# Loading repeated reciprocals from another engine's DMA queue, in smaller groups, in a fused attention and mixture-of-experts kernel

## The reference

```python
x = x + attention(layernorm(x), ctx)          # ctx: 4 x 1601 x 512, 257 image rows, 1344 text rows
# attention: 16 heads of 32
q     = rms_norm(linear(x, q_w), norm_q_w)
k, v  = rms_norm(linear(ctx_txt, k_w), norm_k_w), linear(ctx_txt, v_w)
ki,vi = rms_norm(linear(ctx_img, k_img_w), norm_k_img_w), linear(ctx_img, v_img_w)
out   = linear(softmax(q k^T / sqrt(32)) v + softmax(q ki^T / sqrt(32)) vi, o_w)
x = x + moe(layernorm(x))                     # router, 32 experts, 4 per token, shared expert
```

## Time and profile before

| | us |
|---|---|
| time, median of 3 runs (lowest, highest) | 1255.73 (1253.97, 1257.35) |
| the profiled execution: its time | 1254.77 |
| the profiled execution: its span | 1253.0 |
| PE busy | 1132.6 (90%) |
| DVE busy | 823.3 (66%) |
| ACT busy | 647.8 (52%) |
| POOL busy | 194.9 (16%) |
| mean granted clock of PE | 0.976 of full speed |

### The profile page before, as it was taken

The page is one execution under the profiler, slowest core; times in us unless marked ns, Lnnn a source line. Parts: engine busy times, 40 slices in busy tenths (PEclk is TensorE's granted clock), DMA queues, the critical chain, the costliest instruction groups (busy, mean ns, idle before and its releaser), DMA issues. The chain is left out here.

```text
span 1253.0 us, 20692 instructions
## 1 busy us (share of the span) xinstructions
PE 1132.6 (90%) x8420; PEld 406.4 (32%) x8420; DVE 823.3 (66%) x1034; ACT 647.8 (52%) x916; POOL 194.9 (16%) x299
## 2 busy tenths in 40 slices
PE   7999999779999986989998699999589999999996
PEld 2442223334222233422223242222244434333332
DVE  6766779677677967867787686998468953211221
ACT  5559885334898643489864348996121111211221
POOL 1220000133000022300002240001020003222442
PEclk9999999989999998999999899999889999999999
DMA  9760002557200165720006575013753217999842
GB/s 310 167 119 22 2 2 80 127 105 195 59 2 2 49 140 110 191 76 2 2 22 160 108 191 169 2 35 108 229 216 117 84 78 268 364 303 306 245 70 31
DMA packets 142169, 152.47 MB, mean 122 GB/s; under 512 B 108528, under 2 KB 108784, under 8 KB 136048
## 3 DMA queue, kind: packets, MB, share of 16 engines
q1 hardware_dynamic: 136944, 140.22, 38.4%
q0 software_dynamic: 5120, 10.82, 4.7%
HBM read 104.06 MB, written 21.77 MB: 100 GB/s over the span
## 5 line engine op out<-in xcount | busy, mean ns | idle before, releaser
L705 ACT ACTIVATE work<-ps 128x1024 f32<-128x1024 f32 (+1 forms) x416 | 403.2, 1021 | 42.9 <-PE ps L1178 39.3
L1035 PE MATMUL ps<-wts,work 128*128 128x512 f16 x864 | 203.6, 392 | 43.7 <-DVE work L762 43.4
L1184 PE MATMUL ps<-work,vals 128*32 128x512 f32 (+2 forms) x1664 | 221.0, 603 | 1.8 <-ACT work L705 0.6
L1178 PE MATMUL ps<-quer,keys 32*128 32x512 f16 x2496 | 171.9, 377 | 19.5 <-ACT work L705 5.6
L944 DVE TENSOR_TENSOR work<-work 128x2048 f32<-128x2048 f32 x64 | 146.6, 2291 | 6.2 <-ACT work L705 0.6
L944 DVE TENSOR_TENSOR attn<-attn,work 128x2048 f32<-128x2048 f32 x62 | 142.0, 2291 | 5.5 <-ACT work L705 0.6
L1035 PEld LDWEIGHTS ps<-wts,work 128*128 128x128 f16 x864 | 85.4, 100 | 157.1 <-issue 61.8
L627 ACT CAST work<-work 128x512 f16<-128x512 f32 x68 | 42.0, 618 | 153.8 <-DVE work L794 153.8
L1989 PE MATMUL ps<-wring,xgt 128*80 128x512 f32 x256 | 114.9, 592 | 0.0
L1035 PE MATMUL ps<-wts,hl 128*128 128x512 f16 x432 | 101.1, 386 | 9.6 <-DVE wts L744 7.0
L543 POOL TENSOR_SCALAR small<-small 128x1 f32<-128x1 f32 x68 | 18.2, 268 | 581.1 <-ACT work L632 581.1
(11 more groups left out here) (209 smaller groups left out, 1277.8 us busy)
## 6 DMA issues: line engine op xcount, KB each, us to landing
wring<-in_wx SPq DMA_DIRECT2D x32, 1536.0 KB, 9.2
raw<-in_ctx SPq DMA_DIRECT2D x52, 256.0 KB, 3.3
rb<-sums_inverse SPq DMA_DIRECT2D x24, 256.0 KB, 4.5
work<-in_x SPq DMA_DIRECT2D x4, 1024.0 KB, 5.8
table<-nums SPq DMA_DIRECT2D x16, 256.0 KB, 2.5
work<-in_x SPq DMA_DIRECT2D x12, 256.0 KB, 4.9
x<-work SPq DMA_DIRECT2D x12, 256.0 KB, 2.6
x2t_rows<-nums SPq DMA_DIRECT2D x12, 256.0 KB, 2.6
```

Source lines behind the costliest of these rows:

```text
L705: act.activation(prob[0:rows, s % PROBS, 2 * half:2 * half + 2, :], ps[0:rows, 2 * pair:2 * pair + 2, :], ACT.Exp, scale=SCALE).then_inc(a ...
L1035: mm = pe.matmul(out, lhs(a, c)[:, cols], wts[:, w, z, c * D:(c + 1) * D], start=(k == 0), stop=(k == len(steps) - 1))
L1178: mm = pe.matmul(ps[:, 2 * pair + h % 2, :], k[h * HD:(h + 1) * HD, :], q[h * HD:(h + 1) * HD, :], start=(e == 0), stop=(e == len(terms) - 1))
L1184: return pe.matmul(ps[h * HD:(h + 1) * HD, NUM, :], vals[a:z, ORDER[n], g * P + h * HD:g * P + (h + 1) * HD], prob[a:z, s % PROBS, h, :], ...
```

## The change

The loads of the repeated reciprocals leave SP's order. For the batches 1 to 3 they are issued by ScalarE, one group (512 KB, four DMAs of 128 KB) at a time: groups 0 and 1 in slot 1, between `key_high(0)` and `key_square(1)`, behind a wait for the landed store; group 2 in slot 4, behind `out_high(0)`; group 3 in slot 5, behind `out_high(1)`. `out_high(g)` waits for the multiplication of group g, so the room in `rb` is free. Each of the two halves of `rb` has its own semaphore. The bytes are the same.

For the last batch SP stores the reciprocals and waits for them before the branch, and issues the eight loads at the start of the second program's block, four ahead of the router's weights and four behind. The waits for them inside the branch that is not taken are gone. Each repeated row of these loads is written as one run, 4 KB per partition in `rb` and 8 KB in `rbl`, where it was four of 2 KB.

To free a semaphore, the small loads `ob`, `vb`, `vib`, `mark` count on `s_vq`, behind a wait of SP for the two loads that used it before. `sums_inverse` has room for 4 batches instead of 8.

```diff
-            def spread_pair(bb, q, pair):
-                if pair == 0:
-                    sp.wait_ge(s_zero, 32)
-                    sp.wait_ge(s_rd, 16 * bb)
-                    upto(sp, a_at, q * NG)
-                else:
-                    sp.wait_ge(a_at, gn(q, 1))
-                spread(rb[:, :, :, :], bb - 1, pair, s_rb)
-
-            def last_spreads(bb):
-                store_sums(bb)
-                sp.wait_ge(s_rd, 16 * (bb + 1))
-                for pair in range(2):
-                    spread(rbl[:, 2 * pair:2 * pair + 2, :, :], bb, pair, s_rl[pair])
...
-                            load_vec(OB, "ob", s_vo)
+                            sp.wait_ge(s_vq, 32)
+                            load_vec(OB, "ob", s_vq)
...
-                        if i in (1, 5) and b > 0:
-                            spread_pair(bb, q, i // 4)
...
-                last_spreads(bb)
+                store_sums(bb)
+                sp.wait_ge(s_rd, 16 * (bb + 1))
...
+            def spread(bb, g):
+                for h in range(4):
+                    rows = r_dram[(bb - 1) % B][h * HD + 2 * g:h * HD + 2 * g + 2, :].rearrange("r q -> (r q)")
+                    act.dma_start(rb[h * HD:(h + 1) * HD, g % 2, :, :].rearrange("p t q -> p (t q)"),
+                                  rows.unsqueeze(0).to_broadcast([HD, 2 * L])).then_inc(s_rb[g % 2], 16)
...
+                    if b > 0 and i == 1:
+                        act.wait_ge(s_zero, 32)
+                        act.wait_ge(s_rd, 16 * bb)
+                        spread(bb, 0)
+                        spread(bb, 1)
                     if b > 0 and WEIGH + 1 <= i < WEIGH + 1 + NG:
                         out_high(q, i - WEIGH - 1)
+                        if i - WEIGH - 1 < 2:
+                            spread(bb, i - WEIGH + 1)
...
-                dve.wait_ge(s_rb, 64 * (2 * q + g // 2 + 1))
+                dve.wait_ge(s_rb[g % 2], 64 * (2 * q + g // 2 + 1))
...
+            def spread(pair):
+                for h in range(4):
+                    rows = r_dram[B - 1][h * HD + 4 * pair:h * HD + 4 * pair + 4, :].rearrange("r q -> (r q)")
+                    sp.dma_start(rbl[h * HD:(h + 1) * HD, 2 * pair:2 * pair + 2, :, :].rearrange("p g t q -> p (g t q)"),
+                                 rows.unsqueeze(0).to_broadcast([HD, 4 * L])).then_inc(s_rl[pair], 16)
+
+            spread(0)
             sp.dma_start(rraw[:, :], d["rw"]).then_inc(s_xl, 16)
+            spread(1)
             sp.dma_start(ebias[:, :], d["ebias"].partition_broadcast(P)).then_inc(s_xl, 16)
```

More of the change, by code:

```diff
@@ L387, in store_sums @@
                 sp.wait_ge(a_rcp, bb + 1)
[L388 to L394, removed]
-            def spread_pair(bb, q, pair):
-                if pair == 0:
-                    sp.wait_ge(s_zero, 32)
-                    sp.wait_ge(s_rd, 16 * bb)
-                    upto(sp, a_at, q * NG)
-                else:
-                    sp.wait_ge(a_at, gn(q, 1))
-                spread(rb[:, :, :, :], bb - 1, pair, s_rb)
-            def last_spreads(bb):
-                store_sums(bb)
-                sp.wait_ge(s_rd, 16 * (bb + 1))
-                for pair in range(2):
-                    spread(rbl[:, 2 * pair:2 * pair + 2, :, :], bb, pair, s_rl[pair])
+                sp.dma_start(r_dram[bb % B], rcp[:, :]).then_inc(s_rd, 16)
             def last_loads(p, bb):
@@ L465, in one_pass @@
                             load_weight(WO)
-                            load_vec(OB, "ob", s_vo)
-                            sp.dma_start(vb2[:, 0, :], d["vb"]).then_inc(s_vo, 16)
-                            sp.dma_start(vb2[:, 1, :], d["vib"]).then_inc(s_vo, 16)
-                            sp.dma_start(mark[:, :, :], d["mark"]).then_inc(s_vo, 16)
+                            sp.wait_ge(s_vq, 32)
+                            load_vec(OB, "ob", s_vq)
+                            sp.dma_start(vb2[:, 0, :], d["vb"]).then_inc(s_vq, 16)
+                            sp.dma_start(vb2[:, 1, :], d["vib"]).then_inc(s_vq, 16)
+                            sp.dma_start(mark[:, :, :], d["mark"]).then_inc(s_vq, 16)
                         if bb == 0 and i == 6:
@@ L560, in add_bias @@
                 if q == 0 and j == 0:
-                    pool.wait_ge(s_vo, 64)
+                    pool.wait_ge(s_vq, 96)
                 pool.wait_ge(s_xres[j % 2], 16 * (q * QT // 2 + j // 2 + 1))
@@ L903, in project @@
                     if bb == 0 and i == 12:
-                        dve.wait_ge(s_vo, 64)
+                        dve.wait_ge(s_vq, 96)
                         dve.tensor_tensor(vbias, vb2[:, 0, :], vb2[:, 1, :], ALU.add).then_inc(s_const, 1)
@@ L1304, in _ @@
             with pe.If(pe.value_load(flag[0:1, 0:1], min_val=0, max_val=1) > 0):
-                pe.wait_ge(s_vo, 64)
+                pe.wait_ge(s_vq, 96)
                 one_pass(1)
@@ L1331, in lay_attention, with ffn_program @@
     }
-def ffn_program(nc, m, d, x1_dram, table, out, s_turned, s_rl, s_gate):
+def ffn_program(nc, m, d, x1_dram, table, r_dram, out, s_turned, s_gate):
     with ExitStack() as ctx:
@@ L1366, in ffn_program @@
         s_const, s_i0 = event("s_const"), event("s_i0")
+        s_rl = [event(f"s_rl{i}") for i in range(2)]
         r_lo = event("r_lo")
@@ L2045, in build @@
         s_xr = ctx.enter_context(nc.semaphore("s_xr"))
-        s_rl = [ctx.enter_context(nc.semaphore(f"s_rl{g}")) for g in range(2)]
         s_gate = ctx.enter_context(nc.semaphore("s_gate"))
-        attention_program(nc, m, d, x1_dram, x2_dram, r_dram, table, out, s_turned, s_xr, s_rl, s_gate)
-        ffn_program(nc, m, d, x1_dram, table, out, s_turned, s_rl, s_gate)
+        attention_program(nc, m, d, x1_dram, x2_dram, r_dram, table, out, s_turned, s_xr, s_gate)
+        ffn_program(nc, m, d, x1_dram, table, r_dram, out, s_turned, s_gate)
 def kernel(**inputs):
```

13 lines of the change are left out of this document (5 added, 8 removed).

## The result

The changed kernel takes **1226.2 us** in the median of four runs (1225.1 to 1226.5), the kernel before beside it 1256.1. The ratio is 0.9765, interval 0.9752 to 0.9778: 29.5 us faster. The forecast was 1226.5. The profiled execution took 1225.96 with a span of 1224.2, 28.8 less than the span before. A total that comes out says little about the terms it is made of, so the rest of this text looks at these. Times read from one trace each scatter a little even where the code is the same: the three batches that matter last 633.0, 631.8 and 631.5 us together in the changed kernel, in e1 and in e6.

What follows compares the result with a forecast made beforehand. TensorE, busy 90% of the span, was taken to bound, idling behind loads in SP's queue. B −35.8, A +5.4 and the last batch +1.6 sum to −28.8 us: 1226.0 or 1226.9, written as 1226.5, range 1213 to 1240.

Steps and rivals of the forecast that it cites:

- What bounds: Whole kernel: TensorE, busy 90% of the span, loses time where loads from SP's queue come late.
- B: Slot 5, batches 1 to 3: earlier group 2 load removes TensorE's idle time and low clock before `key(7)`, −35.8 us.
- together at 249.4: At `key(7)`, batch 1: VectorE's work and TensorE itself both allow the start at 249.4, so nothing idles.
- A: Start of projections, batches 1 to 3: wait moves to ScalarE, delaying `key(3)`, while `ctx` tile 4 comes in time; +5.4 us.
- the issue: ScalarE's `rb` loads in slot 1: eight issues at 0.42 us each, taken from SP's four in 1.73 us.
- the low clock: TensorE after an idle stretch: twelve matmuls at the lower clock level, 4.44 us instead of 2.75 in batch 1.
- Rival 3: Batches 1 to 3: loads land no earlier, only SP's issue time is won, 12 us in all, 1244; chance 0.03.
- The last batch: Around the branch: multiply waits 5.0 us longer, earlier code fetch gives back 3.4; net +1.6, from −0.5 to +5.0.
- one sign that was named: Behind the branch: block starts 9 to 11 us after the flag, with a wait of about 5 for `rbl`.
- the bound of 5.5: Behind the branch: code fetch, if it waits for the loads, can begin up to some 5.5 us earlier.
- rival 1: ScalarE's issues cost almost nothing (0.05 us each), `key(3)` starts after 2.9 us idle: 1217; chance 0.17.

Runs made afterwards that it cites:

- e1: Changed kernel with the last batch's eight `rbl` loads back ahead of the branch on SP: 1224.66 us, ratio 0.9759 to the kernel before.
- e6: Changed kernel with four of the last batch's `rbl` loads ahead of the branch, the other four behind it: 1224.12 us, ratio 0.9753.
- e3: Changed kernel with groups 0 and 1 loaded by SP as a pair at the old place in slot 1, groups 2 and 3 on ScalarE: 1223.73 us, 0.9746.
- e5: Changed kernel with all `rb` loads on SP, one group at a time, each behind its slot's `ctx` load from slot 2 on: 1208.83 us, ratio 0.9634.
- e9: Repeat of e5, timed beside e10 on one chip in five rounds: 1206.51 us, ratio 0.9639.
- e8: Changed kernel with ScalarE's wait for the store and eight issues moved from slot 1 to slot 2, ahead of `key_high(1)`: 1216.3 us, ratio 0.9684.
- e2: Kernel before with only the last batch's loads moved behind the branch: 1254.93 us, ratio 1.0003.
- e4: Changed kernel with groups 0 and 1 issued by ScalarE as four DMAs of 256 KB instead of eight of 128 KB: 1220.19 us, ratio 0.9722.
- e7: e5 with four of the last batch's `rbl` loads ahead of the branch and four behind: 1206.47 us, ratio 0.961.
- e10: Repeat of e7, timed beside e9 on one chip in five rounds: 1202.31 us, ratio 0.9612.

## Why the prediction was right, point by point

**What bounds, and the mechanism of B.** Right. The wait for `rb` is gone, group 2 is issued in slot 4 and landed ahead of its use, and the time won at `key(7)` is carried to the end of the batch.

**The size of B, −35.8, was too large.** The step counted TensorE's idle time of the earlier trace rows as the load's. The gain ends at the first other limit: as soon as the load is early, VectorE, late by its wait at tile 4 and 3.49 us away from `key(7)` at `weigh(2)`, bounds. e3 measured −30.8. The text did say that VectorE and TensorE would arrive together at 249.4, which is why the sum came out: with A's delay on TensorE the limit does not bite, since TensorE is as late. The two terms don't add: A costs +3.2 on top of B alone (−30.8 to −27.6), and +8.2 on top of a B counted at TensorE's idle time. The +5.4 of the text stands between; and the forecast for e3, made by adding up A's share and taking it away, failed for it.

**A.** The wait, the eight issues and the engines behind them were right; `key(3)` was forecast at 226.5 and started at 227.53, 0.8 of which is the later start of the frame. Mis-sized were two: the issue (0.49 us each in this group, 0.42 taken from SP's row), and the low clock, taken as some 1.65 us for twelve matmuls, while all twelve matmuls ran low in batch 1 (5.28, 2.5 above) and nearly all in the other two (5.02 and 4.97). Taken together the batches were forecast at −30.4 (−35.8 + 5.4) and came to −27.6: the forecast was 0.7 to 1.2 us too fast in each.

**The rule on issuing engines.** The rule of the Trainium skill in "DMA: Bandwidth & Descriptors", section "Issuing engines are not separate DMA queues", is that issuing from several engines saves only the time of issue. The traces agree with half of it. Rival 3, the saving of issue time alone, is out: 12 us was its gain, 29.5 the measured. But the rule's sense, that another engine is no faster road, held better than the change: e5, with every load on SP, gains 46.0 us by its ratio. What was lost before was lost to how the loads stood in one queue's order, and what the change lost again, to the wait and the issues on an engine that others wait for.

**The last batch.** Forecast +1.6, in the trace +0.1 from flag to multiply. Both halves were too small and offset each other, which is luck: the block starts 7.0 earlier (3.4 taken; the end of the range was 5.5), and the wait for `rbl` is 7.0 (5.0 taken). So one sign that was named failed too: the block was to start 9 to 11 us after the flag and starts 5.3 after it. The step that failed is the bound of 5.5. It counts only how much earlier the fetch can begin, and that part was about right: the first instruction packets come 5.0 us earlier. The other 2.0 arise between the first packets and the block, 5.8 us before and 3.8 after; before, the first group of packets is carried beside the loads and takes until 8.5 us after the flag, 2.0 us from its first packet, where it takes 1.0 in the kernel after. Where the rest of the 2.0 arises is not shown. (SP's last issue ended 1.4 us after the flag, not 1.3; and rival 1, by its own rates, leaves 2.7 us of idle time ahead of `key(3)`, not 2.9. Neither changes a conclusion.)

**What made up the rest.** Batches at −27.6 instead of −30.4 and the last batch at +0.1 instead of +1.6 give −27.5, of a span shorter by 28.8. The 0.78 at the start and the −1.9 behind the flag close it. The latter is no effect of the change that I can show: from flag to end the twelve traces of this case have 365.6 to 373.1 us, and kernels with the same code there differ by 4.5 (e9 368.6, after 370.7, e8 373.1). Where in the experts' part this is decided was not tried. That the forecast of 1226.5 lies within 0.3 us of the time is luck: the batches gained 2.8 less than forecast, and the last batch and the 1.9 behind the flag made up for it.

## What to carry to other kernels

When a list of waits shows a wait for a DMA, look first where the load stands in its queue's order and behind which semaphore, and only then whose queue it is: a group at a time in slots 2 to 5 of SP's own order, behind the `ctx` loads, the same bytes gained 46.0 us, where another engine's queue gained 29.5. An engine that others wait for pays for every DMA that it issues and for every semaphore ahead of it, so if it must issue, let it be few and large ones. And the idle time of the bounding engine at a wait, with what the low clock behind it costs, is an upper bound of what removing this wait alone gives (35.8 counted, 30.8 measured): look up when the next engine of the chain would be ready.

## What the runs showed of the hardware

The start of a block behind a far branch depends on what the DMA engines carry: 5.3 to 5.8 us after the flag with nothing in flight (kernel after, e2, e3, e4, e5, e8, e9), 6.9 to 7.6 with 1 MB (e7, e10, e6), 11.9 and 12.3 with 2 MB (e1, before). With 2 MB in flight no instruction packet was carried in the first 6 us after the flag (e1 and before), while the loads used all of the 16 engines' time; with nothing in flight the first came after 1.5 us. Loads ahead of a branch are thus not hidden by it; half of them ahead and half behind was best here.

A DMA issued by ScalarE took 0.31 to 1.57 us, 0.44 in the median of 48, and the trace has no other instruction of ScalarE in slot 1's stretch of eight; in a group of eight it was 0.49 each, in a group of four 0.44, for twice the bytes.

The low clock level after an idle stretch is not a matter of the stretch's length alone. In e4 TensorE ran the twelve matmuls of `key(3)` in 4.37 us after 3.04 us of idle time in batch 2, and in 2.75, the high level throughout, after 3.01 in batch 3; in the kernel before they took 4.41 after 9.91 us and 5.28 after 9.65.
